# Cross attention on one core: scores issued in 17 visits a group on two sets of three banks, other products cut into 32-column tiles, V in a ring of 18 tiles

## The chip, the cores and the metric

One Trainium2 chip, one NeuronCore. The metric is the device time of one execution in microseconds (us), float32 throughout.

## The reference, cut to what matters

Eight batches; 512 queries, 1593 text keys (padded to 1600) and 8 image tokens; 20 heads of 16 dimensions.

```python
q = split_heads(hidden_states @ w_q)          # (8, 20, 512, 16)
k = split_heads(text @ w_k); v = split_heads(text @ w_v)      # text: (8, 1593, 512)
out_text = softmax(q k^T / sqrt(16)) v
out_ip = softmax(q k_ip^T / sqrt(16) + mask_ip) v_ip          # 8 tokens a batch
out = (out_text + out_ip) @ w_out + b_out + hidden_states
```

## The kernel before, in words

Heads are worked in groups of four (`GH`), five groups a batch, 40 groups in all. K and Q of a group are made in float32, split into a high and a low part by GpSimd, stored to a scratch tensor and loaded again as stacks of 48 rows, two heads on partitions 0 to 47 and two on 64 to 111 (`SIDE`). With these stacks the scores are made twice, with single-pass matmuls (`exact`, float32r).

- **Maxima.** `max_unit` (L540) makes scores with queries on the partitions, one matmul for each side; `take_max` (L851) reduces the pair on VectorE. 32 units of 2 x 400 columns are made for each group, one group ahead. `max_bank` has four banks, so two units are in flight: unit u waits for the reduction of unit u - 2. `negative_parts` (L856) negates the maxima and splits them; `negative_piece` (L494) transposes them on TensorE; `negative_copy` (L728) copies them on ScalarE and issues two DMAs into rows 48 and 49 of `q_stack`, from ScalarE's queue. The next group's exponent scores wait for them (`neg_loaded`, L650).
- **Exponents.** `exp_tile` (L554) makes scores with keys on the partitions, the negated maximum riding along as two more rows, and ScalarE takes the exponent out of PSUM (L741 to L754). 50 tiles a group, two banks. The last two tiles (`k_tail`, L569) use both sides at once.
- **Values.** `pv_tile` (L572) multiplies the four heads' probabilities with `v_ones`, each head in its own 32-column part of the array (17 columns used), 13 key tiles a group. A float32 matmul appears in the trace as two passes, so one `pv_tile` is 8 matmuls.
- **Other products** (`work`, L498) share one bank, `work_bank`: `k_piece` (L440, 64 columns wide, two halves side by side), `q_piece` (L451), `v_piece` (L471, 128 columns wide), `out_piece` (L486), `ip_piece` (L462), the folded image weights (WA, WB) and the transposes TA, TB.

TensorE's order is written by hand. The loop of `body` (L637) goes over 13 key tiles `kt`; each has maximum units, two exponent tiles, maximum units, `pv_tile` of `kt - 1`, two more exponent tiles, maximum units and a share of `work` from `work_plan` (L62). So the array goes from scores to values, back to scores, to other work, and back. All engines run the same plan in order.

- VectorE: reductions, and between them `invert_sums` (L867), which waits for the DMA of the sums, `ip_scale` (L842), `out_add` (L896) and the two halves of the image softmax (L872, L885).
- SyncE's queue, in `body` L397: `normalise` (L353: sums out, reciprocals to scratch, broadcast back), `pack` (L363), and `stack_group` (L342) for the group after next: store K, wait, load K (12 DMAs), store Q, load Q. `normalise` stands ahead of the K loads.
- ScalarE's queue: the four context loads of the next batch (`load_ctx`, L761, 3.3 MB) behind the copy of K piece (4, 1), at visit (2, 3); x after Q piece 4; and the maxima's DMAs at `kt` 12 of each group.
- In the prologue (L602 to L635) K and Q of groups 0 and 1 and the first six V tiles are made, with the 32 maximum units of group 0 beside.

Of the kernel before, what the change touches and what calls it, by code (L numbers as in the profile page):

```python
# [40 lines left out]
QUARTERS = 4  # L41
EXPS = FULL * GH + GH // 2
UNITS = (GH // SIDES) * QT * QUARTERS
BLOCKS = (0, 0, 1)
Q_BLOCKS = (0, 1, 0)
LOADS = SIDES * (2 * len(BLOCKS) + len(Q_BLOCKS))
SCALE = float(DH) ** -0.5
NEG = -10000.0
GRID_W, GRID_H = 32, 16
V_EARLY = 6  # L50


def share(steps, turn):

    n, m = turn
    return range(steps * n // m, steps * (n + 1) // m)


WHOLE = (0, 1)


def work_plan(first, last):  # L62

    turns = {("Q", 2): (0, 0), ("K", 2, 0): (0, 1, 2), ("K", 2, 1): (0, 3, 4), ("IP", 2): (0, 5),
             ("K", 3, 0): (1, 0, 1), ("K", 3, 1): (1, 2, 3), ("Q", 3): (1, 4), ("IP", 3): (1, 5), ("K", 4, 0): (1, 12),
             ("K", 4, 1): (2, 0, 1, 2, 3), ("Q", 4): (2, 4, 5, 6), ("IP", 4): (2, 7), ("WA",): (2, 9), ("WB",): (2, 10, 11),
             ("TA",): (3, 10), ("TB",): (3, 11)}
    turns.update({("V", t): (0, t) for t in range(V_EARLY, KT)})  # L70
    if not first:
        turns.update({("OUT", 0): (1, 6, 7), ("OUT", 1): (1, 8, 9), ("OUT", 2): (1, 10), ("OUT", 3): (1, 11)})
    if not last:
        turns.update({("K", 5, 0): (2, 12), ("K", 5, 1): (3, 0, 1, 2, 3), ("Q", 5): (3, 4), ("IP", 5): (3, 5),
                      ("Q", 6): (3, 6, 7, 8), ("IP", 6): (3, 9), ("K", 6, 0): (3, 12), ("K", 6, 1): (4, 0, 1)})
        turns.update({("V", t): (4, 2 * t + 2, 2 * t + 3) for t in range(V_EARLY - 1)})
        turns["V", V_EARLY - 1] = (4, KT - 1)
    else:

        turns.update({("WB",): (2, 12), ("TA",): (3, 11), ("TB",): (3, 12)})  # L80
    plan = {}
    for piece, (g, *kts) in turns.items():
        for n, kt in enumerate(kts):
            assert (g, kt) not in plan
            plan[g, kt] = (piece, (n, len(kts)))
    return plan
# [6 lines left out]
def ends(turn):  # L93
    return turn is not None and turn[0] == turn[1] - 1

SPLITS = ((("Q", 2), ("K", 2, 0), ("K", 2, 1)), (("K", 3, 0), ("K", 3, 1), ("Q", 3)),
# [6 lines left out]
def work_order(first, last):  # L105

    plan, order = work_plan(first, last), {}
    for g in range(NG):
        for kt in range(KT):
            if kt == NEG_AT and not (last and g == NG - 1):  # L110
                order["NEG", g + 1] = len(order)
# [1000 lines left out]
```

## Time and profile before

| | us |
|---|---|
| runs | 2120.46, 2136.64, 2138.08; median 2136.64 |
| profiled execution, its own time | 2130.14 |
| its span, first to last instruction | 2128.3 |
| mean granted TensorE clock | 0.978 |

The span is what a profile shows; the execution's own time lies 1.8 us above it. In the rows below, PE is TensorE's matmuls and PEld its weight loads, DVE is VectorE, ACT is ScalarE; SPq and ACTq are the instructions that issue DMAs.

### The profile page before, as it was taken

The numbers are of one execution on the slowest core, as the hardware profiler recorded it, in microseconds if no ns is written. First come the engines' busy times: TensorE is split into PE (matmuls) and PEld (weight loads), VectorE is DVE, ScalarE is ACT, GpSimd is POOL, SyncE is SP. The second block draws the span as 40 slices with busy tenths as digits, with TensorE's granted clock in tenths as the row PEclk, the third lists the DMA queues.
The fourth block names the chain that finished last, engine by engine and source line by source line (L and its number), as shares of the span: only waits on it lengthen the run. The fifth ranks groups of instructions, "written<-read, shape, count | busy, mean of one in ns | idle before, by whom it ended". The sixth has DMA issues, their size and how long they took to land.

```text
span 2128.3 us, 31016 instructions
## 1 busy us (share of the span) xinstructions
PE 2011.5 (95%) x12048; PEld 824.6 (39%) x12048; DVE 1341.9 (63%) x1623; ACT 1231.1 (58%) x2364; POOL 275.6 (13%) x314
## 2 busy tenths in 40 slices
PE   4899999997999999999999999999999999999987
PEld 2443334432344333443334433444334443344332
DVE  4757666565665676666755667656766567666660
ACT  0256566555565566555655566655666556665665
POOL 3001111101111011111111111011110111111100
PEclk8999899999999999999999999999999999999999
DMA  7234433353333544435333353333533344443301
GB/s 196 53 53 84 112 67 74 74 117 75 63 76 71 129 81 76 76 66 144 68 70 72 68 141 61 73 61 73 134 66 76 64 119 90 83 77 67 74 21 41
DMA packets 94309, 174.86 MB, mean 82 GB/s; under 512 B 37937, under 2 KB 62386, under 8 KB 90322
## 3 DMA queue, kind: packets, MB, share of 16 engines
q1 hardware_dynamic: 86066, 144.55, 35.1%
q10 hardware_dynamic: 7936, 28.18, 3.9%
q8 instruction: 95, 1.56, 0.3%
q14 instruction: 52, 0.43, 0.1%
q0 software_dynamic: 160, 0.14, 0.1%
HBM read 117.75 MB, written 48.82 MB: 78 GB/s over the span
## 4 chain that ended last, share of the span: by engine, by line
PE 84%; DMA 4%; issue 4%; ACT 4%; DVE 2%; ACTq 1%; SPq 1%; POOL 0%; POOLq 0%
PE pv_bank L580 22%; PE exp_bank L566 19%; PE max_bank L548 14%; PE work_bank L474 10%; PE work_bank L445 10%; PE work_bank L489 3%; PE work_bank L455 3%; DMA q_stack<-neg_rows 3%; ACT probs L754 2%; DVE quarter_max L853 1%; PE work_bank L467 1%; ACT probs_tail L754 1%; ACTq L738 1%; ACTq L763 1%; DMA ctxt<-in_ctx_t 0%
## 5 line engine op out<-in xcount | busy, mean ns | idle before, releaser
L853 DVE TENSOR_REDUCE quarter_max<-max_bank 128x2 f32<-128x800 f32 x1280 | 1232.4, 989 | 692.0 <-PE max_bank L548 687.7
L754 ACT ACTIVATE probs<-exp_bank 128x512 f32<-128x512 f32 x1872 | 1016.2, 595 | 528.3 <-PE exp_bank L566 501.0
L548 PE MATMUL max_bank<-k_stack,q_stack 48*128 48x400 f32 x2560 | 542.7, 384 | 55.9 <-issue 28.2
L566 PE MATMUL exp_bank<-q_stack,k_stack 50*128 50x512 f32 x1872 | 507.3, 469 | 19.9 <-ACT probs L754 19.7
L580 PE MATMUL pv_bank<-probs,v_ones 128*17 128x512 f32 x3840 | 512.5, 606 | 2.0 <-ACT probs L754 2.0
L566 PEld LDWEIGHTS exp_bank<-q_stack,k_stack 50*128 50x128 f32 x1872 | 227.9, 186 | 501.6 <-ACT probs L754 473.5
L548 PEld LDWEIGHTS max_bank<-k_stack,q_stack 48*128 48x128 f32 x2560 | 271.8, 189 | 244.7 <-issue 105.5
L445 PE MATMUL work_bank<-ctxt,wk 128*64 128x400 f32 x1280 | 257.8, 523 | 12.9 <-DMA ctxt<-in_ctx_t 11.1
L474 PE MATMUL work_bank<-wv,ctxt 128*128 128x320 f32 x768 | 246.1, 455 | 0.4 <-ACT neg_rows L698 0.4
L996 POOL TENSOR_TENSOR k_parts<-k_full,zero 128x400 fp32r<-128x400 f32 x80 | 68.2, 852 | 930.4 <-ACT k_full L698 930.4
L474 PEld LDWEIGHTS work_bank<-wv,ctxt 128*128 128x128 f32 x768 | 136.3, 191 | 85.5 <-issue 39.9
L1025 POOL TENSOR_TENSOR o_sum<-o_sum,r_wide 128x512 f32<-128x512 f32 x40 | 51.0, 1276 | 654.0 <-DMA r_wide<-scratch_r 654.0
L698 ACT ACTIVATE v_ones<-work_bank 128x320 f32<-128x320 f32 (+1 forms) x112 | 46.9, 419 | 152.2 <-PE work_bank L474 131.3
L445 PEld LDWEIGHTS work_bank<-ctxt,wk 128*64 128x64 f32 x1280 | 79.2, 139 | 140.4 <-issue 118.0
L580 PEld LDWEIGHTS pv_bank<-probs,v_ones 128*17 128x17 f32 x3840 | 63.8, 95 | 144.8 <-issue 120.7
L698 ACT ACTIVATE k_full<-work_bank 128x400 f32<-128x400 f32 x80 | 40.4, 505 | 135.0 <-PE work_bank L445 135.0
L999 POOL TENSOR_TENSOR k_parts<-k_full,k_parts 128x400 fp32r<-128x400 f32 x80 | 83.1, 1039 | 6.3
L455 PE MATMUL work_bank<-xt,wq 128*64 128x256 f32 (+1 forms) x480 | 72.5, 405 | 0.6 <-ACT k_full L698 0.6
L489 PE MATMUL work_bank<-wout,o_t 128*128 128x320 f32 (+1 forms) x224 | 71.6, 452 | 0.0
L1004 POOL TENSOR_TENSOR q_parts<-q_full,zero 128x256 fp32r<-128x256 f32 x40 | 24.5, 612 | 232.0 <-DMA scratch_q<-q_parts 140.5
L754 ACT ACTIVATE probs_tail<-exp_bank 128x512 f32<-128x512 f32 x78 | 42.3, 596 | 11.5 <-PE exp_bank L569 11.0
L489 PEld LDWEIGHTS work_bank<-wout,o_t 128*128 128x128 f32 (+1 forms) x224 | 39.1, 189 | 24.0 <-issue 12.8
(86 smaller groups left out, 585.4 us busy)
## 6 DMA issues: line engine op xcount, KB each, us to landing
k_stack<-scratch_k SPq DMA_DIRECT2D x240, 200.0 KB, 6.1
scratch_k<-k_parts SPq DMA_DIRECT2D x80, 400.0 KB, 4.7
ctxt<-in_ctx_t ACTq DMA_DIRECT2D x28, 800.0 KB, 9.1
q_stack<-scratch_q SPq DMA_DIRECT2D x240, 64.0 KB, 2.3
scratch_q<-q_parts SPq DMA_DIRECT2D x80, 128.0 KB, 6.7
r_wide<-scratch_r SPq DMA_DIRECT2D x40, 256.0 KB
o_t<-o_sum SPq DMA_DIRECT2D x160, 32.0 KB, 2.0
xres<-in_x SPq DMA_DIRECT2D x8, 640.0 KB, 4.3
```

The costliest lines, as they stand in the source:

```text
L445: last = nc.tensor.matmul(work_bank[half * GR:(half + 1) * GR, 0:CHUNK], wk[:, ct, (g % NG) * GR:(g % NG + 1) * GR], ctxt[:, ct, keys:keys ...
L455: last = nc.tensor.matmul(work_bank[half * GR:(half + 1) * GR, 0:QHALF], wq[0:rows, ct, (g % NG) * GR:(g % NG + 1) * GR], xt[0:rows, ct, h ...
L474: last = nc.tensor.matmul(work_bank[:, 0:D], ctxt[:, ct, t * 128:(t + 1) * 128], wv[:, ct, :], start=(ct == 0), stop=(ct == CT - 1))
L489: last = nc.tensor.matmul(bank, o_t[0:rows, k, t * 128:(t + 1) * 128], wout[0:rows, k, :], start=(k == 0), stop=(k == k_end))
L548: last = nc.tensor.matmul(max_bank[:, (u % 2) * 2 + side, 0:CHUNK], exact(q_stack[stack, slot, c, t * 128:(t + 1) * 128]), exact(k_stack[s ...
L566: nc.tensor.matmul(bank[:, :], exact(k_stack[stack, slot, c, kt * 128:(kt + 1) * 128]), exact(q_stack[stack, slot, c, :]), start=True, sto ...
L580: last = nc.tensor.matmul(pv_bank[h * 32:h * 32 + VW, :], v_ones[:, kt, head * VW:(head + 1) * VW], p, start=(kt == 0), stop=(kt == FULL))
L698: return nc.scalar.activation(dst, src, ACT.Copy)
L754: nc.scalar.activation(dst, exp_place(n, final), ACT.Exp, scale=SCALE).then_inc(probs_ready, 1)
L853: nc.vector.reduce_max(quarter_max[:, :, u // QUARTERS, u % QUARTERS], max_bank[:, (u % 2) * 2:(u % 2) * 2 + 2, 0:CHUNK], AX.X).then_inc(m ...
L996: nc.gpsimd.tensor_tensor(exact(part[:, 0, :]), k_full[:, c, :], zero[:, :].to_broadcast([128, CHUNK]), ALU.add)\
L999: nc.gpsimd.tensor_tensor(exact(part[:, 1, :]), k_full[:, c, :], part[:, 0, :], ALU.subtract).then_inc(k_split, 1)
```

## The change

- The scores of a group go in 17 visits (`VISITS`). A visit makes three exponent tiles on three banks and three maximum tiles of 512 columns on three banks, exponent and maximum by turns on opposite sides. `exp_bank` has three banks, `max_bank` three instead of four, and `begin_round` waits until VectorE has reduced *all* of the round before. A maximum round is one reduction of 3 x 512 (`take_max`); round 0 is `max_rest`, 16 matmuls of 64 columns for the last 64 keys. So 17 rounds a group in place of 32 units.
- Maxima run a group and two rounds ahead (`LEAD`): visit 14 has the last round of the next group, visit 15 the transposition, and visit 15 also round 0 of the group after.
- Behind the scores of a visit come `pv_tile` (in 13 of 17 visits, `PV_AT`) and then the other work, both in 32-column parts of the array: `strips` cuts K, Q, V, OUT, IP, WA, WB, TA, TB to 32 columns, up to four side by side. Transposes become float32 matmuls with the identity; the third step of Q is padded to 128 rows.
- V in a ring of 18 tiles, ten made in the batch before; K made three groups ahead (K 7 in group 4); probabilities in a ring of three.
- SyncE's queue in a group is now: load K of the group after next, `normalise`, `pack`, store and load Q, and last `store_k(group_no + 3)`. K piece (4, 1), and so the context load behind it, ends in visit 14 of group 1. `invert_sums` stands at visit 2 of each group, the softmax halves at (2, 5) and (2, 12).
- The prologue makes K of group 2 and V tiles 0 to 9, with 19 rounds beside.

```diff
+BANKS = 3
+VISITS = FULL * GH // BANKS + 1
+ROUNDS = VISITS
+LEAD = 2
+V_RING = 18
+V_EARLY = 10
+PV_AT = {0: FULL, 2: 0, 3: 1, 4: 2, 6: 3, 7: 4, 8: 5, 10: 6, 11: 7, 12: 8, 14: 9, 15: 10, 16: 11}
+NEG_AT = 15
...
+    put(1, ("K", 4, 0), 4, (11, 2), (12, 2))
+    put(1, ("K", 4, 1), 4, (13, 3), (14, 1))
...
-                    if g or not first:
+                    if group_no + 2 < B * NG:
+                        slot_free(group_no + 2)
+                        load_k(group_no + 2)
+                    if group_no:
                         normalise(group_no - 1)
...
+                    if group_no + 3 < B * NG:
+                        store_k(group_no + 3)
...
+            def strips(rows):
+                return [(at, min(32, rows - at)) for at in range(0, rows, 32)]
...
+                        for at, rows in strips(GR):
+                            dims = (g % NG) * GR + at
+                            last = nc.tensor.matmul(work_bank[half * GR + at:half * GR + at + rows, 0:CHUNK],
+                                                    wk[:, ct, dims:dims + rows], ctxt[:, ct, keys:keys + CHUNK],
+                                                    start=(ct == 0), stop=(ct == CT - 1))
...
+            def begin_round(n, r):
+                if r == 0:
+                    pe.wait_ge(stack_loaded[n % RING], loads_of(n))
+                if n * ROUNDS + r:
+                    pe.wait_ge(max_taken, n * ROUNDS + r)
...
+                    for v in range(VISITS):
+                        n, r = round_at(group_no, v)
+                        if v == 0 or v == VISITS - 1:
+                            if n is not None:
+                                max_round(n, r)
+                            if v == 0:
+                                pe.wait_ge(neg_loaded, (group_no + 1) * 32)
+                            for at in tiles_at(v):
+                                exp_tile(group_no, at)
+                        else:
+                            for k, at in enumerate(tiles_at(v)):
+                                exp_tile(group_no, at)
+                                if n is not None and r:
+                                    if k == 0:
+                                        begin_round(n, r)
+                                    max_tile(n, r, k)
+                            if n is not None and r == 0:
+                                max_round(n, r)
...
+            def take_max(n, r):
+                dve.wait_ge(max_scores, n * EXPS + SIDES + r * BANKS)
...
+                nc.vector.reduce_max(out_at, scores, AX.X).then_inc(max_taken, 1)
```

## Rows read from the trace of the kernel before

**Rows 1.** The page, busy time, share of the span and instructions.

```profile
PE 2011.5 (95%) x12048; PEld 824.6 (39%) x12048; DVE 1341.9 (63%) x1623; ACT 1231.1 (58%) x2364; POOL 275.6 (13%) x314
```

**Rows 2.** Six middle batches (first, last, sum): length, busy times, clock, DMA share, GB/s.

```profile
343.00:610.00 267.00, 250.08 (x1501) 102.31 (x1498) 165.29 (x200) 153.92 (x295) 32.96 (x38) 0.97 0.40 81
...
1626.00:1878.00 252.00, 244.50 (x1492) 100.31 (x1493) 165.25 (x200) 153.20 (x294) 33.08 (x38) 1.00 0.41 85
sum 1535.00, PE 1484.00 PEld 607.58 DVE 991.77 ACT 922.20 POOL 198.22; mean PE 247.33 PEld 101.26 DVE 165.30 ACT 153.70 POOL 33.04
```

**Rows 3.** Groups of instructions: busy us, mean ns of one, idle before.

```profile
L853 DVE TENSOR_REDUCE quarter_max<-max_bank 128x2 f32<-128x800 f32 x1280 | 1232.4, 989 | 692.0 <-PE max_bank L548 687.7
L754 ACT ACTIVATE probs<-exp_bank 128x512 f32<-128x512 f32 x1872 | 1016.2, 595 | 528.3 <-PE exp_bank L566 501.0
...
L880 DVE TENSOR_REDUCE ip_max<-s_ip 128x80 f32<-128x640 f32 x8 | 6.6, 820 | 0.3
```

**Rows 4.** TensorE's waits: us in total, times, longest.

```profile
PE max_bank L548 <- DVE quarter_max L853: 12.4, 15, 1.2
```

**Rows 5.** Timeline, one key tile with a K piece: start us, us, what.

```profile
885.34 1.56 PE L445 MATMUL work_bank<-ctxt,wk 128*64 128x400 f32 x8
...
886.83 0.46 PE L548 MATMUL max_bank<-k_stack,q_stack 48*128 48x400 f32 x2
...
887.12 0.40 PE L566 MATMUL exp_bank<-q_stack,k_stack 50*128 50x512 f32 x2
...
887.36 0.35 PE L548 MATMUL max_bank<-k_stack,q_stack 48*128 48x400 f32 x2
...
887.64 1.05 PE L580 MATMUL pv_bank<-probs,v_ones 128*17 128x512 f32 x8
...
888.63 0.57 PE L566 MATMUL exp_bank<-q_stack,k_stack 50*128 50x512 f32 x2
```

**Rows 6.** Timeline, a V tile and the matmul behind it.

```profile
892.50 2.42 PE L474 MATMUL work_bank<-wv,ctxt 128*128 128x320 f32 x8
...
894.86 0.46 PE L548 MATMUL max_bank<-k_stack,q_stack 48*128 48x400 f32 x2
```

**Rows 7.** Timeline, scores to reduction (two places), and reduction to scores.

```profile
1005.53 0.34 PE L548 MATMUL max_bank<-k_stack,q_stack 48*128 48x400 f32 x2
...
1005.92 0.99 DVE L853 TENSOR_REDUCE quarter_max<-max_bank 128x2 f32<-128x800 f32 x1 [0.60 <-PE max_bank L548]
...
64.76 2.79 DVE L853 TENSOR_REDUCE quarter_max<-max_bank 128x2 f32<-128x800 f32 x3 [0.50 <-PE max_bank L548]
65.81 0.19 PEld L548 LDWEIGHTS max_bank<-k_stack,q_stack 48*128 48x128 f32 x2 [1.24 <-DVE quarter_max L853]
```

**Rows 8.** Timeline, SyncE's queue, last K loads and behind them; then a sums DMA alone.

```profile
901.68 1.35 SPq L329 DMA_DIRECT2D k_tail<-scratch_k  x3
903.08 1.23 SPq L310 DMA_DIRECT2D scratch_q<-q_parts  x2
910.20 1.95 SPq L339 DMA_DIRECT2D q_stack<-scratch_q  x2
...
2080.18 1.93 DMA sums<-o_sum
```

**Rows 9.** Context loads: from issue to landing.

```profile
DMA to landing us min/median/max: 4.9/8.5/14.2
```

**Rows 10.** Timeline, one group whose stack came late, with the idle time before.

```profile
508.65 0.70 PE L548 MATMUL max_bank<-k_stack,q_stack 48*128 48x400 f32 x2 [9.76 <-issue]
```

**Rows 11.** Timeline, where the parts of the kernel begin: V, exponents, the end.

```profile
59.20 2.50 PE L474 MATMUL work_bank<-wv,ctxt 128*128 128x320 f32 x4
...
91.85 0.39 PE L566 MATMUL exp_bank<-q_stack,k_stack 50*128 50x512 f32 x2
...
2107.70 0.59 SPq L356 DMA_DIRECT2D sums<-o_sum  x1
```

**Rows 12.** Timeline, 80 short matmuls in a row.

```profile
22.91 3.24 PE L589 MATMUL work_bank<-probs 128*64 128x64 f32 x80 [0.87 <-DMA probs<-in_w_v_ip]
```

More of the change, by code:

```diff
@@ L108, in work_order @@
     for g in range(NG):
-        for kt in range(KT):
-            if kt == NEG_AT and not (last and g == NG - 1):
+        for v in range(VISITS):
+            if v == NEG_AT and not (last and g == NG - 1):
                 order["NEG", g + 1] = len(order)
-            piece, turn = plan.get((g, kt), (None, None))
+            piece, turn = plan.get((g, v), (None, None))
             if begins(turn):
@@ L532, in work @@
                     for t in range(QT):
-                        last_mm = nc.tensor.transpose(work_bank[:, t * 128:(t + 1) * 128], p_ip[:, t, 0:128], ident_f[:, :])
+                        for at, rows in strips(128):
+                            last_mm = nc.tensor.matmul(work_bank[at:at + rows, t * 128:(t + 1) * 128],
+                                                       p_ip[:, t, at:at + rows], ident_f[:, :], start=True, stop=True)
                     last_mm.then_inc(work_full, 1)
@@ new lines, in max_tile @@
+            def max_tile(n, r, k):
+                i, slot = (r - 1) * BANKS + k, n % RING
+                side, at, chunk = i % SIDES, i // (SIDES * CHUNKS), i // SIDES % CHUNKS
+                c, t = at // QT, at % QT
+                stack = slice(side * SIDE, side * SIDE + STACK)
+                nc.tensor.matmul(max_bank[:, k, :], exact(q_stack[stack, slot, c, t * 128:(t + 1) * 128]),
+                                 exact(k_stack[stack, slot, c, chunk * WIDE:(chunk + 1) * WIDE]),
+                                 start=True, stop=True).then_inc(max_scores, 1)
@@ new lines, in max_rest @@
+            def max_rest(n):
+                slot = n % RING
+                for at in range(PAIRS):
+                    c, t = at // QT, at % QT
+                    for side in range(SIDES):
+                        stack = slice(side * SIDE, side * SIDE + STACK)
+                        mm = nc.tensor.matmul(max_bank[:, side, at * TAIL:(at + 1) * TAIL],
+                                              exact(q_stack[stack, slot, c, t * 128:(t + 1) * 128]),
+                                              exact(k_stack[stack, slot, c, CHUNKS * WIDE:KEYS]), start=True, stop=True)
+                        if at == PAIRS - 1:
+                            mm.then_inc(max_scores, 1)
@@ L600, in ip_values @@
                 last.then_inc(work_full, 1)
-            units = iter(range(UNITS))
+            rounds = iter(range(ROUNDS + LEAD))
             pe.wait_ge(wk_loaded, 16)
@@ L945, in _ @@
             dve.wait_ge(mask_step, step + 3)
-            units = iter(range(UNITS))
+            rounds = iter(range(ROUNDS + LEAD))
             for piece, turn, beside in PRO_PLAN:
@@ L984, in _ @@
             for t in range(QT):
[L985 removed]
+                out_add(B, t, end + t, out_place(t))
         @block.gpsimd
@@ L1043, in _ @@
                 split_q(g, PRO_ORDER["Q", g])
+            for c in range(2):
+                split_k(2, c, PRO_ORDER["K", 2, c])
             def body(b, first, last):
```

483 lines of the change are left out of this document (243 added, 240 removed).

## Prediction

> **What bounds the kernel now.** I read the page's busy times first: TensorE 95%, VectorE 63%, ScalarE 58% [rows 1]. Then the same by batches: in the middle six TensorE is busy 247 of 256 us. An undisturbed one is 252 us long; the first of the six is 267 us, some 10 of them lost at one late stack [rows 2, 10]. TensorE's waits say the same from the other side: it waited for VectorE's reductions 12.4 us in all [rows 4]. So TensorE's order of work is the kernel, and every idle stretch that the change opens in it is paid in full.
>
> The timeline shows what TensorE's time is made of [rows 5]. Scores: a first pair of 400 columns starts at 886.83, a pair of 512 at 887.12, the next at 887.36, the values at 887.64. A pair of 512 columns therefore takes 0.24 us from start to start; the first one after a change of form 0.10 more (its weights are not loaded ahead), and on leaving 0.10 more (the array empties). The values: 887.64 to 888.63, 0.99 us, of which two passes of 512 columns stream 0.43 us each and about 0.13 is again entering and leaving. K: 0.33 us a pass (1.49 us for four passes and the switch). V: 2.36 us for 8 passes, 0.27 each and 0.2 at the ends [rows 6]. Each key tile pays four such switches, some 0.2 us each.
>
> **What the change takes from TensorE.** The streamed columns stay the same: four 32-column tiles side by side move at the rate of the values' four. Per middle batch of 85 visits I get:
> - scores: a visit has three pairs of 512 columns, 0.33 + 0.24 + 0.33 = 0.90 us. Visit 15 has the rest round, eight pairs of 64 columns limited by their 128-column weights at 0.11 each, 1.6 us; visit 16 the tails, 1.3 us. 15 x 0.90 + 2.9 = 16.4 a group, 82 us;
> - values 65 x 0.85 = 55.5;
> - K 40 steps x 0.67 = 26.7, V 52 x 0.53 = 27.7, output 16 x 0.53 = 8.5, Q 15 x 0.43 = 6.4, the small ones 7;
> - entering and leaving the 32-column form once a visit, 85 x 0.13 = 11.
>
> Sum 225 us against 252: 11% less. What it could cost more: four times as many instructions. 80 matmuls with their loads ran at 0.04 us each [rows 12]; a K step is 8 in 0.67 us, a V step 8 in 0.53, so their issue is covered; only TA, TB and IP may be issue bound (under 1 us a batch either way).
>
> The Trainium skill (TensorEngine Tiling (Array Packing), Key Properties) says that changing the tiling mode drains the array; the 0.10 us on leaving the scores [rows 5] agrees.
>
> **The wait that is added.** Before, a unit waited for the reduction two units back. Now `begin_round` waits for the reduction of the round just before: all three banks are filled, reduced, and only then filled again. The cycle, from rows: after VectorE's end TensorE's next load starts 0.06 us later (65.75 to 65.81, [rows 7]); weights and two further matmuls of the same side until the third maximum starts, 0.11 + 2 x 0.23 = 0.57; from a matmul's start to VectorE's, 0.39 at 400 columns (1005.53 to 1005.92, [rows 7]), 0.43 at 512; the reduction: 800 elements take 0.989 us [rows 3], 0.83 of it at 0.96 elements per ns and 0.16 fixed, so 1536 take 1.76. Sum 2.8 us. Bounds on the reduction: 1.60 without its fixed part, 1.90 in proportion to the 800.
>
> Visits last 225 / 85 = 2.64 us on average, but unevenly: a visit with only values or only two small steps has 1.9 to 2.5 us of work, one with four steps 3.2 or more, visits 15 and 16 3 to 4. In-order issue means that nothing is caught up: whatever is behind the first maximum (the values and the work of that visit) waits too. Walking the 85 visits with this recurrence gives idle time of 5.8, 3.6, 6.7, 4.6 and 4.2 us in the five groups (the 6.7 has 1.8 at (2, 7), where the softmax, three operations of 0.82 us [rows 3], holds back a reduction). 225 + 25 = 250 us: nearly all of the gain is gone.
>
> The Trainium skill (Perfetto Trace Analysis, Optimizing Scalar/DVE Operations) speaks against this edit: where VectorE isn't saturated but causes bubbles on other engines, instructions should be broken up; here they are merged. VectorE at 63% [rows 1] is such a case, and by this rule too TensorE gets bubbles.
>
> **Two transfers behind others in a queue.** (a) SyncE now issues the 12 K loads ahead of the sums. Twelve issues take 5.4 us (1.35 for three, [rows 8]); a store issued behind them let its waiter go at 910.20, 7.1 us after its issue at 903.08, while a sums DMA alone takes 1.9 [rows 8]. VectorE waits for the sums at visit 2, 8.4 us into the group, and behind it stands the reduction that the maxima of visit 4 need. K loads can begin once the group before has made its last scores, 2 us before the group, where K was stored early (groups 3, 4, 0): sums there at 9 to 10 us, 0.7 us lost each. After group 0 K is stored late (piece (3, 1) ends at visit 14): 2.9 us lost in group 1. Bounds a group: 0 if the sums overtake, 5 if they take the full 7 us.
> (b) The context load now is issued at the end of visit 14 of group 1, and the next thing on ScalarE's queue is the DMA of the maxima of group 2, in visit 15. The last of four context loads lands up to 14.2 us after its issue [rows 9]. If a queue serves in order, the maxima land 15 to 16 us after visit 14; TensorE wants them 6 us after it (visits 15, 16 and three maxima). 9 to 10 us idle in seven batches; bounds 1 (no order: ScalarE is still 2 us late by issuing the four) and 12. I take 9.7: the least and the largest landing of the four loads, 4.9 and 14.2 us [rows 9], look like a queue, and a late stack can cost as much, 9.76 us [rows 10]. In the batch with that stop the granted clock was 0.97, in the undisturbed one 1.00 [rows 2]: 3% of a batch is 7 us, the nearest row for a stop of this length; I take 3 us a batch, since the low clock partly falls on idle time.
>
> The Trainium skill (DMA: Bandwidth & Descriptors, Two DMAs through the same engine are not ordered) says that within a queue of one DMA engine descriptors start in order; no row here shows a small DMA behind the context load.
>
> **The sum.** A middle batch: 250 + 2 (groups 3, 4, 0) + 2.9 + 9.7 + 3 + 1.5 of other waits = 269 us. Prologue: values of V start near 58 as now [rows 11]; 17 rounds of 2.8 us, then the negated maxima and two more visits, 58 + 47 + 8 = 113 us until the first exponent, against 92. Last batch: 49, 49, 50, 45 and a last group bound by ScalarE, 50 x 0.595 [rows 3] = 30, with 10 of late sums and 3 of the rest: 237. The end is as before, 21 us from the sums [rows 11] and 2 ahead of them. 113 + 7 x 269 + 237 + 23 = **2256 us**, against the profiled 2130, which lies 0.3% under the median of the runs.
>
> **Rivals.**
> - *No queue effect* (sums and maxima overtake the loads): batches of 254, 113 + 7 x 254 + 228 + 23 = 2142. For it: the 16 DMA engines are only 41% busy [rows 2]. Against: the 7.1 us behind the K loads. Chance 0.14.
> - *TensorE stays the bound*, the other side: the three reductions hide under values and work. It decides at a loop of 2.64 us, 0.16 less than I add up, or if exponent tiles absorb the wait; with 225 + 6 a batch: 105 + 7 x 231 + 215 + 23 = 1960. For it: VectorE's total falls, 17 reductions of 1.7 against 32 of 1. Against: the loop leaves at most 1.9 us of each 2.8 to VectorE, and light visits can't borrow. Chance 0.16.
> - *The tiles don't do what they say*: 32-column pieces of K, V and output run two abreast, not four. That doubles 63 us a batch: 8 x 63 on top of the forecast, above 2700. The values' eight matmuls in 0.99 us speak against it. Chance 0.03.
> - *More of (a) and (b)*: 12 us in (b) and 5 in each group for (a), 20 us more a batch: 2400. Chance 0.07.
>
> The forecast itself, 2190 to 2340, has 0.60; without half of (a) and (b) it is the lower end, with three fifths of the last rival's 20 us the upper. A difference of 1% is about what a measurement of this kernel can tell from none. Slower by over 1%: 0.60 + 0.03 + 0.07 and a small part of the first rival, 0.73; within: 0.10; faster 0.17. The range: 2085 to 2380, which takes in the first rival and most of the last, and leaves out the second and third, 0.19.
>
> **What would show it.** TensorE's waits: maxima for VectorE's reduction some 150 to 200 us in all, in most visits 0.2 to 0.9 us each; visits in the timeline never under 2.8 us; segments of V in 2.14 us without ends; reductions of 1.75 us. Once a batch, at the start of group 2, a stop of near 10 us for the maxima's DMA, and at visits 2 to 4 of group 1 VectorE idle for the sums. Wrong would be: TensorE busy over 95% again, no stop at group 2, a visit of 2.4 us.

## Result: 2330 us, 9.3% slower, and the profile after

The changed kernel takes 2329.9 us (median of 4 runs, 2328.3 to 2335.3) against 2135.7 (2120.5 to 2138.1) in the same comparison: ratio 1.093, 95% interval 1.088 to 1.098. The forecast was 2256 in a range of 2085 to 2380, so 5.6% slower where it is 9.3%. The profiled execution spans 2326.9 us. Here and below a time is the median of the fast runs; the one slow run (2620.2 us, of the last experiment) is left out. The page of the profiled execution, against [rows 1], first busy times, then the granted clock in 40 slices:

```profile
PE 2082.4 (89%) x17944; PEld 829.8 (36%) x17944; DVE 1294.7 (56%) x1025; ACT 1223.8 (53%) x2364; POOL 281.0 (12%) x314
...
PEclk9998999999999899998999899998999989999777
```

TensorE fell from 95% to 89% of a longer span. Its busy time rose by 71 us although the streamed columns are the same. Part of the stream ran at the lower clock: the mean granted clock of the run is 0.938, against 0.978 before. VectorE and ScalarE lost share too, so every engine now waits.

The middle batches, from first exponent to first exponent (the first of six, and the sum of the six; columns as in [rows 2]):

```profile
380.65:659.53 278.88, 254.40 (x2233) 102.05 (x2231) 158.90 (x125) 152.65 (x296) 33.77 (x38) 0.95 0.37 77
...
sum 1664.24, PE 1519.50 PEld 610.59 DVE 953.39 ACT 916.82 POOL 202.64; mean PE 253.25 PEld 101.76 DVE 158.90 ACT 152.80 POOL 33.77
```

A batch takes 277.4 us (1664.24 / 6) where an undisturbed one took 252 [rows 2], and the forecast had 269. TensorE is busy 253.3 of it and idle 24.1; the granted clock of the six lies between 0.95 and 0.97.

TensorE's waits, the place of [rows 4], and VectorE's for the sums:

```profile
PEld max_bank L596 <- DVE tile_max L918: 207.1, 272, 5.5
DVE recips L935 <- DMA sums<-o_sum: 171.8, 39, 35.4
PE max_bank L596 <- DVE tile_max L918: 110.0, 175, 5.2
PE exp_bank L632 <- DMA q_stack<-neg_rows: 50.2, 9, 7.6
```

The first and third row are one wait, seen by the weight load and by the matmul: where [rows 4] had 12.4 us for TensorE, there are 110. The stops for the sums, below, are in these 110 too, since what TensorE then waits for is a reduction. The other two are the two transfers of the forecast.

Now the timeline of a group 1, visits 2 to 4. The single wait a round, as it repeats:

```profile
716.00 0.56 PE L596 MATMUL max_bank<-k_stack,q_stack 48*128 48x512 f32 x2
...
717.01 1.76 DVE L918 TENSOR_REDUCE tile_max<-max_bank 128x3 f32<-128x1536 f32 x1 [0.54 <-PE max_bank L596]
...
718.82 0.19 PEld L596 LDWEIGHTS max_bank<-k_stack,q_stack 48*128 48x128 f32 x2 [0.22 <-DVE tile_max L918]
718.82 0.51 PE L596 MATMUL max_bank<-k_stack,q_stack 48*128 48x512 f32 x2
```

From 716.00 to 718.82 is the loop: 2.82 us with a reduction of 1.76 in it, as added up. In the last two rows the weight load waited 0.22 us, while the matmul shows no idle time: a part of this wait is hidden in TensorE's busy time. And the stop for the sums behind it:

```profile
718.56 0.60 SPq L381 DMA_DIRECT2D sums<-o_sum  x1
...
724.18 0.25 DVE L935 RECIPROCAL recips<-sums 128x16 f32<-128x16 f32 x1 [5.41 <-DMA sums<-o_sum]
724.35 1.70 DVE L918 TENSOR_REDUCE tile_max<-max_bank 128x3 f32<-128x1536 f32 x1
...
726.10 0.80 PE L596 MATMUL max_bank<-k_stack,q_stack 48*128 48x512 f32 x2 [4.37 <-DVE tile_max L918]
```

VectorE stands 5.41 us at the reciprocal with a reduction of maxima ready behind it, and TensorE stands 4.37 at the maxima that need that reduction. The stretches before and after it (length, busy times, granted clock):

```profile
711.00:721.30 10.30, 10.30 (x97) 4.12 (x93) 5.76 (x4) 7.25 (x15) 0.00 (x0) 1.00 0.90 123
726.10:729.50 3.40, 3.40 (x17) 1.31 (x21) 1.72 (x1) 1.08 (x2) 0.00 (x0) 0.50 0.27 93
729.50:733.00 3.50, 3.50 (x30) 1.25 (x26) 0.68 (x3) 0.65 (x2) 1.27 (x1) 0.64 0.09 32
```

Ahead of the stop the clock is granted in full (2.4 GHz), behind it half (1.2 GHz) for 3.4 us and partly for 3.5 more. Over those 6.9 us this costs 3.4 x 0.50 + 3.5 x 0.36 = 3.0 us of TensorE's work. By this estimate a stop of 4.4 us costs over 7.

Last, the start of group 2:

```profile
764.19 1.24 SPq L336 DMA_DIRECT2D scratch_k<-k_parts  x2
...
765.58 1.30 ACTq L800 DMA_DIRECT2D q_stack<-neg_rows  x2
...
774.58 1.22 PE L632 MATMUL exp_bank<-q_stack,k_stack 50*128 50x512 f32 x3 [6.88 <-DMA q_stack<-neg_rows]
774.66 1.23 SPq L358 DMA_DIRECT2D k_stack<-scratch_k  x3
...
780.12 0.59 SPq L381 DMA_DIRECT2D sums<-o_sum  x1
```

The maxima let TensorE go 9.0 us after their issue. The K store, issued in the same two microseconds on the other queue, lets the K loads go 10.5 us after its own.

### The profile page after: what moved, and what is told of

The parts are those of the page before. It is cut to its first block, busy times and chain, and to the rows that moved or that the text cites. A ratio compares the mean times of both kernels' runs of the same rounds, so it can differ in the third digit from the quotient of the medians.

```text
span 2326.9 us, 42217 instructions
## 1 busy us (share of the span) xinstructions
PE 2082.4 (89%) x17944; PEld 829.8 (36%) x17944; DVE 1294.7 (56%) x1025; ACT 1223.8 (53%) x2364; POOL 281.0 (12%) x314
## 4 chain that ended last, share of the span: by engine, by line
PE 55%; DMA 17%; DVE 13%; SPq 9%; issue 3%; POOL 1%; ACT 1%; POOLq 0%; ACTq 0%
PE pv_bank L648 13%; DMA sums<-o_sum 11%; DVE tile_max L918 11%; PE exp_bank L632 11%; PE max_bank L596 11%; PE work_bank L475 9%; PE work_bank L508 6%; DMA scratch_k<-k_parts 5%; SPq L361 4%; SPq L358 4%; PE work_bank L524 2%; PE max_bank L607 1%; POOL k_parts L1066 1%; POOL k_parts L1063 1%; PE exp_bank L636 1%
## 5 line engine op out<-in xcount | busy, mean ns | idle before, releaser
L918 DVE TENSOR_REDUCE tile_max<-max_bank 128x3 f32<-128x1536 f32 (+1 forms) x680 | 1173.0, 1725 | 801.0 <-PE max_bank L596 769.5
L596 PE MATMUL max_bank<-k_stack,q_stack 48*128 48x512 f32 x1920 | 596.2, 464 | 110.6 <-DVE tile_max L918 110.0
L632 PE MATMUL exp_bank<-q_stack,k_stack 50*128 50x512 f32 x1920 | 600.3, 451 | 52.3 <-DMA q_stack<-neg_rows 50.2
L632 PEld LDWEIGHTS exp_bank<-q_stack,k_stack 50*128 50x128 f32 x1920 | 273.7, 196 | 420.1 <-ACT probs L817 208.2
L475 PE MATMUL work_bank<-ctxt,wk 128*32 128x400 f32 x2560 | 257.7, 507 | 21.1 <-DMA ctxt<-in_ctx_t 11.0
L508 PE MATMUL work_bank<-wv,ctxt 128*32 128x320 f32 x3072 | 254.6, 445 | 15.3 <-DVE s_ip L904 14.2
L508 PEld LDWEIGHTS work_bank<-wv,ctxt 128*32 128x32 f32 x3072 | 97.1, 112 | 175.8 <-issue 73.6
L475 PEld LDWEIGHTS work_bank<-ctxt,wk 128*32 128x32 f32 x2560 | 77.7, 111 | 186.2 <-issue 162.0
L1071 POOL TENSOR_TENSOR q_parts<-q_full,zero 128x256 fp32r<-128x256 f32 x40 | 24.5, 611 | 664.3 <-ACT q_full L757 661.0
L817 ACT ACTIVATE probs_tail<-exp_bank 128x512 f32<-128x512 f32 x80 | 43.4, 595 | 94.5 <-PE exp_bank L636 85.8
L524 PE MATMUL work_bank<-wout,o_t 128*32 128x320 f32 (+1 forms) x928 | 80.3, 467 | 0.0
L486 PE MATMUL work_bank<-xt,wq 128*32 128x256 f32 x960 | 71.0, 401 | 1.2 <-ACT k_full L757 1.2
```

Source lines behind the costliest of these rows:

```text
L475: last = nc.tensor.matmul(work_bank[half * GR + at:half * GR + at + rows, 0:CHUNK], wk[:, ct, dims:dims + rows], ctxt[:, ct, keys:keys + C ...
L508: last = nc.tensor.matmul(work_bank[at:at + rows, 0:D], ctxt[:, ct, key:key + rows], wv[:, ct, :], start=(ct == 0), stop=(ct == CT - 1))
L524: last = nc.tensor.matmul(bank[at:at + rows, :], o_t[0:deep, k, t * 128 + at:t * 128 + at + rows], wout[0:deep, k, :], start=(k == 0), sto ...
L596: nc.tensor.matmul(max_bank[:, k, :], exact(q_stack[stack, slot, c, t * 128:(t + 1) * 128]), exact(k_stack[stack, slot, c, chunk * WIDE:(c ...
L632: nc.tensor.matmul(bank[:, :], exact(k_stack[stack, slot, c, kt * 128:(kt + 1) * 128]), exact(q_stack[stack, slot, c, :]), start=True, sto ...
L817: nc.scalar.activation(dst, exp_bank[:, at % BANKS, :], ACT.Exp, scale=SCALE).then_inc(probs_ready, 1)
```

## Experiments

"A batch" below is the mean of the six middle ones in the run's profile. The changed kernel: first exponent at 102.1, a batch 277.4, last batch 257.5. The kernel before, run beside each set of experiments, had medians of 2133 to 2140 us; between experiments of different sets a difference under 10 us shows nothing by itself.

**The sums ahead of the K loads.**

```diff
-                    if group_no + 2 < B * NG:
-                        slot_free(group_no + 2)
-                        load_k(group_no + 2)
                     if group_no:
                         normalise(group_no - 1)
+                    if group_no + 2 < B * NG:
+                        slot_free(group_no + 2)
+                        load_k(group_no + 2)
```

> The sums' DMA is issued ahead of the 12 K loads again, as before the change; nothing else differs from the changed kernel. If the late sums (landing 7 us after issue behind the loads) hold VectorE and through it TensorE, they now land about 1.9 us after issue, the visits 3 and 4 of each group fall to the loop's 2.8 to 3.1 us, and 1.6 us in each of groups 3, 4 and 0, 6.7 in group 1 and 4 in group 2 go: 15 us a batch, 2210 us in all. Rival A: it is the loop alone that holds those visits, then less than 15 us go. Rival B: the K loads, now issued behind the sums' whole round trip, come too late for the next group's maxima, then the time rises above 2330.

Measured 2183.4 us (2179.1 to 2186.0), 1.019 of the kernel before (1.017 to 1.022); a batch 259.4. The gain, 147 us, is more than the 120 expected, 18.0 us a batch and not 15; the clock of the whole run rose from 0.938 to 0.963. In the six middle batches together:

```profile
sum 1556.47, PE 1475.68 PEld 605.27 DVE 953.60 ACT 916.67 POOL 202.51; mean PE 245.95 PEld 100.88 DVE 158.93 ACT 152.78 POOL 33.75
```

TensorE is busy 246.0 us a batch and not 253.3, and idle 13.5 and not 24.1, at a granted clock of 0.98. So of the 18.0 us some 10.7 were idle time, and 7.3 the same work at the lower clock. In a group 1 the reciprocal now starts with no idle time before it, right behind a reduction:

```profile
676.42 1.76 DVE L918 TENSOR_REDUCE tile_max<-max_bank 128x3 f32<-128x1536 f32 x1 [0.55 <-PE max_bank L596]
678.10 0.24 DVE L935 RECIPROCAL recips<-sums 128x16 f32<-128x16 f32 x1
```

Rival A falls, as more than 15 us a batch went. Rival B falls as well: the K loads behind the sums are in time.

**The sums as late, but VectorE at them later.** `INVERT_AT = 2` becomes `INVERT_AT = 6`, all else as in the changed kernel.

> The changed kernel, queue orders as it has them, but VectorE inverts the sums at visit 6 of a group, not at visit 2: the sums stay as late as they are, only VectorE's reductions no longer stand behind the wait. If the price of the late sums is VectorE's wait and nothing else, the time is that of the run with the sums issued first, 2183, or up to 20 us over it; the DMA of the sums still lands some 7 us after its issue. Rival: the late sums cost by what follows them (scaling, packing, the next store and load of Q), or the K loads ahead are what cost; then it stays near 2330.

Measured 2182.0 us (2181.6 to 2191.2), a batch 259.4: the same as with the sums first. As ratios to the kernel before the two are 1.025 (1.022 to 1.028) and 1.019, so they agree to 0.6%. In a group 1 the sums' DMA is issued as late as ever, and nothing waits:

```profile
679.72 0.60 SPq L381 DMA_DIRECT2D sums<-o_sum  x1
...
691.29 0.24 DVE L935 RECIPROCAL recips<-sums 128x16 f32<-128x16 f32 x1
```

So the price of the late sums is VectorE's wait with the reductions queued behind it, and within 0.6% nothing after it. Two unlike edits, one on SyncE's queue and one number in VectorE's order, give the same 147 us.

**The context load behind the maxima's DMA.**

```diff
                         if v == NEG_AT and group_no + 1 < B * NG:
                             negative_copy(...)
+                            if g == 1 and not last:
+                                load_ctx(b + 1)
...
                             k_copy(b * NG + piece[1], piece[2], number)
-                            if piece == ("K", 4, 1) and not last:
-                                load_ctx(b + 1)
```

> The context load is issued one visit later, behind the DMA of the maxima of group 2 on ScalarE's queue; nothing else differs from the changed kernel. If the context load is what makes the maxima late, they land in 2.6 us as in the other groups, the stop at the start of group 2 goes (7 us with the late last visit of group 1, in seven batches, and up to 3 us of clock): 2260 to 2280 us. Rival: the maxima are late because all 16 DMA engines are full with K loads and stores, whichever queue they are on; then their landing stays near 9 us and the time within 10 us of 2330.

Measured 2357.3 us (2349.8 to 2364.9), 1.101 of before (1.098 to 1.104, the changed kernel 1.093): 27 us slower than the changed kernel, a batch 281.7, neither what the theory nor what its rival said. The stop at the start of group 2 did shrink, the last visit of group 1 from 9.5 to 5.5 us. But visit 3 of group 2 now took 13 to 15 us:

```profile
1064.31 0.62 SPq L381 DMA_DIRECT2D sums<-o_sum  x1
1077.63 0.25 DVE L935 RECIPROCAL recips<-sums 128x16 f32<-128x16 f32 x1 [10.92 <-DMA sums<-o_sum]
```

The context load and the 12 K loads are now under way together, and the sums behind the K loads land 13.3 us after their issue. The stop moved from one small transfer to the other.

**Both orders undone.** The two diffs above together.

> Both queue orders undone. If the two costs are separate, their gains add: about 2150 us, and what is left against the kernel before (2136) is the loop of one wait per round and the longer prologue. Rival: the two stops cover each other or something else becomes late behind them, then it stays over 2200.

Measured 2156.1 us (2153.1 to 2162.9), 1.008 of before (1.005 to 1.010), as expected; a batch 254.8. With the sums out of reach, moving the context load gives 27 us, as many as it cost without. The two gains are not separate: that of the second edit changes its sign with the first.

This order has a smaller stop of its own, which is not for a transfer:

```profile
710.02 4.40 ACTq L826 DMA_DIRECT2D ctxt<-in_ctx_t  x4
...
715.27 1.19 PE L632 MATMUL exp_bank<-q_stack,k_stack 50*128 50x512 f32 x3 [2.83 <-ACT probs_tail L817]
```

ScalarE spends 4.40 us on issuing the four context loads, and the last exponents of group 1 stand behind it. TensorE waits 2.83 us for them at the start of group 2, in each of seven batches.

**The maxima by another queue.** On top of the sums' order, the DMA of the maxima is issued by SyncE (ScalarE only copies them out of PSUM), the context load staying at visit 14; first behind the store of K:

```diff
                         store_k(group_no + 3)
+                    if group_no + 1 < B * NG:
+                        sp.wait_ge(work_empty, number(("NEG", g + 1)) + 1)
+                        for side in range(SIDES):
+                            ...
+                            sp.dma_start(q_stack[...], neg_rows[...]).then_inc(neg_loaded, 16)
```

> As the run with the sums issued ahead of the K loads (2183), the context load at its place at visit 14, but the DMA of the maxima goes by SyncE's queue, behind the store of K, and not by ScalarE's behind the context load. If what makes the maxima late in group 2 is that they stand behind the context load in one queue, they land in 3 to 5 us, the last visit of group 1 falls from 9.5 to 5 or 6 us and the time to about 2156 us, as with the context load issued behind them. Rival: the 16 DMA engines are full with the context load whichever queue it came by; then the maxima land near 9 us still, and the time stays near 2183.

Measured 2193.1 us (2188.8 to 2194.9), a batch 260.4: no gain. The maxima land as late as on ScalarE's queue, 8.9 us from issue to matmul. But the store of K stood ahead of them, so that the place in a queue was not excluded. The second time the same lines stand ahead of the store:

> As the run with the maxima's DMA on SyncE's queue (2193), but issued ahead of the store of K, so that nothing large stands ahead of it in its own queue; the context load is issued 4 us earlier by ScalarE's queue. If the place in a queue decides, the maxima of group 2 now land in 3 to 4 us, the last visit of group 1 takes 5 to 6 us and the time is about 2156 to 2165 us. If the 16 DMA engines are simply full with the context load, they land 7 to 9 us after issue, that visit stays over 9 us and the time stays at 2185 to 2200 us.

Measured 2171.4 us (2166.3 to 2174.4), between the two, 12 us less than with ScalarE's queue (2183.4). As ratios, 1.017 (1.011 to 1.022) and 1.019 (1.017 to 1.022), the two can't be told apart; but a batch is 257.4 and not 259.4. Both runs in the timeline, first behind the store, then ahead of it:

```profile
718.07 1.24 SPq L336 DMA_DIRECT2D scratch_k<-k_parts  x2
719.36 1.43 SPq L456 DMA_DIRECT2D q_stack<-neg_rows  x2
...
728.28 1.22 PE L639 MATMUL exp_bank<-q_stack,k_stack 50*128 50x512 f32 x3 [6.70 <-DMA q_stack<-neg_rows]
```

```profile
716.67 1.45 SPq L454 DMA_DIRECT2D q_stack<-neg_rows  x2
718.16 1.29 SPq L336 DMA_DIRECT2D scratch_k<-k_parts  x2
...
724.08 1.22 PE L639 MATMUL exp_bank<-q_stack,k_stack 50*128 50x512 f32 x3 [5.31 <-DMA q_stack<-neg_rows]
```

With nothing large ahead in its own queue the small DMA still needs 7.4 us from issue to matmul. The last visit of group 1 takes 9.5 us behind the context load, 7.9 ahead of the K store, 5.5 with the context load behind. The place in the queue is worth the first 1.6 us. The other 2.4 aren't all the transfer's: with the context load ahead, ScalarE copies the maxima 1.9 us after the last matmul of their transposition has started, held up by issuing the loads (2.1 to 2.2 us); with the load behind it is 0.3 us. By an estimate from these, 1.6 us of the 5.31 that TensorE waits above are the late copy, and 3.7 the landing, though nothing large stood ahead in the queue. Nor is 5.5 a visit without a stop, since the 2.83 us for ScalarE are in it. By the Trainium skill (DMA: Bandwidth & Descriptors, Issuing engines are not separate DMA queues) transfers from any issuing engine run on the same 16 DMA engines and interleave; the slow landing on a queue of its own agrees.

**One reduction a bank.** Queue orders as in the changed kernel.

```diff
                 stack = slice(side * SIDE, side * SIDE + STACK)
+                pe.wait_ge(max_taken, n * TAKES + (1 if r == 1 else 1 + (r - 2) * BANKS + k + 1))
                 nc.tensor.matmul(max_bank[:, k, :], ...
...
-                nc.vector.reduce_max(out_at, scores, AX.X).then_inc(max_taken, 1)
+                    for k in range(BANKS):
+                        at = i % (SIDES * CHUNKS) + k
+                        dve.wait_ge(max_scores, n * EXPS + SIDES + i + k + 1)
+                        nc.vector.reduce_max(flat[:, at:at + 1], max_bank[:, k, :], AX.X).then_inc(max_taken, 1)
```

> Each round's reduction is cut into three of 512 elements, one a bank, and TensorE waits for a bank's own reduction only; queue orders as in the changed kernel. If the single wait a round (the loop of 2.8 us) holds light visits, visits with 2 us of work now take 2.2 us, and 20 us a batch go: about 2180 us, although VectorE has 34 instructions more a group and about 0.3 us more work a visit (3 x 0.69 = 2.08 against 1.73). Rival A: VectorE's instructions are the limit, then nothing goes or the time rises. Rival B: the late sums and maxima take over what the loop leaves (they stand on the same path); then only half goes, 2250 us.

Measured 2190.3 us (2187.1 to 2193.7), 1.023 of before: 140 us less, where 150 were expected. That the total fits is partly luck: a batch takes 264.9 us, 12.5 less and not 20. The first exponent at 94.5 (7.6 earlier) and the last batch of 225.4 (32 shorter) make up for it. In the middle batches the stops for the sums take up part of the gain, as rival B had it: visit 3 of the groups 0 and 2 to 4 takes 5.2 to 6.9 us (medians), where it took 4.2 to 4.8.

**All three together.**

> Both queue orders undone and each round's reduction cut into three, one a bank. If the late sums and maxima and the one wait a round are together all that stands between the changed kernel and its TensorE work (225 us a batch worked out), a middle batch now takes 230 to 237 us, the first exponent comes at 94.5 as with the cut reductions alone, and the whole takes 1965 to 2000 us, well under the kernel before. Rival: TensorE's work, with four times as many instructions in 32-column pieces, is itself some 240 to 250 us a batch, then 2050 to 2110.

Measured 1945.7 us (1938.2 to 1947.4), ratio to the kernel before 0.914, 95% interval 0.911 to 0.917. It beats both kernels. First exponent at 93.1, a batch 231.9, last batch 207.7. Its page, a middle batch, the group of reductions and the wait that is left:

```profile
PE 1880.2 (97%) x17944; PEld 762.1 (39%) x17944; DVE 1365.4 (70%) x2305; ACT 1195.5 (61%) x2364; POOL 281.9 (14%) x314
```

```profile
1480.89:1712.81 231.92, 228.76 (x2233) 92.99 (x2231) 167.76 (x285) 149.19 (x296) 33.94 (x38) 0.99 0.47 93
```

```profile
L598 PE MATMUL max_bank<-k_stack,q_stack 48*128 48x512 f32 x1920 | 621.8, 442 | 5.0 <-DVE tile_max L921 3.2
```

TensorE waits 3.2 us for reductions in the whole kernel, though VectorE does three instructions where it did one, and 71 us more in all. TensorE is the bound again, at 97%. The run to compare with is the one with both orders undone, whose wait and middle batches are:

```profile
PE max_bank L596 <- DVE tile_max L918: 66.4, 145, 2.7
```

```profile
sum 1528.80, PE 1473.82 PEld 604.52 DVE 953.65 ACT 916.31 POOL 202.55; mean PE 245.64 PEld 100.75 DVE 158.94 ACT 152.72 POOL 33.76
```

A batch falls from 254.8 to 231.9, by 22.9 us, at the same granted clock of 0.99. Only 6.0 of them were shown as idle time (9.2 and 3.1 a batch); 16.9 stood in TensorE's busy time, 245.6 and 228.8. The same visit in both, exponent and maximum, first with one wait a round, then with one a bank:

```profile
878.69 0.50 PE L632 MATMUL exp_bank<-q_stack,k_stack 50*128 50x512 f32 x1
879.09 0.50 PE L596 MATMUL max_bank<-k_stack,q_stack 48*128 48x512 f32 x2
```

```profile
793.64 0.50 PE L634 MATMUL exp_bank<-q_stack,k_stack 50*128 50x512 f32 x1
793.64 0.73 PE L598 MATMUL max_bank<-k_stack,q_stack 48*128 48x512 f32 x2
```

The maximum starts 0.40 us behind the exponent in one and with it in the other, and neither shows idle time. The list of waits understates a short wait that recurs.

What the prediction draws from the Trainium skill (Perfetto Trace Analysis, Optimizing Scalar/DVE Operations), that an unsaturated engine which causes bubbles elsewhere should have its instructions broken up, is what these rows show.

**What the 32-column pieces are worth.** In that fastest version `strips` returns `[(0, rows)]`.

> As the run before it in this list, with K, Q, V, output and the small products undivided again (one matmul of 64 or 128 columns of weights where there were two or four of 32). If the 32-column pieces save only switches of the array's form (0.13 to 0.2 us in each of some 78 visits a batch that have other work), this costs 10 to 16 us a batch: 80 to 130 us over that run. Rival A: the pieces save nothing, the same within 10 us. Rival B: the pieces cost (their issue is not covered), then this one is faster.

Measured 2037.2 us (2030.1 to 2044.5): 91 us more, a batch 243.8 and not 231.9, so 11.9 us for 85 visits. It is still 96 us under the kernel before (2133.2): of the 187 us that the fastest version gains, the pieces give about a half, and the visits and the prologue the rest. The same visit in both, values, a K step and the next scores; with the pieces, then without:

```profile
748.92 1.05 PE L650 MATMUL pv_bank<-probs,v_ones 128*17 128x512 f32 x8
749.79 0.85 PE L476 MATMUL work_bank<-ctxt,wk 128*32 128x400 f32 x8
750.58 0.50 PE L634 MATMUL exp_bank<-q_stack,k_stack 50*128 50x512 f32 x1
```

```profile
783.35 1.05 PE L650 MATMUL pv_bank<-probs,v_ones 128*17 128x512 f32 x8
784.33 0.89 PE L476 MATMUL work_bank<-ctxt,wk 128*64 128x400 f32 x4
785.15 0.49 PE L634 MATMUL exp_bank<-q_stack,k_stack 50*128 50x512 f32 x1
```

Values to K takes 0.87 us within one form of the array and 0.98 across two; the K step itself 0.79 against 0.82. That is 0.14 us in this visit; in each of 85 it would be the 11.9.

**The pieces alone, in the kernel before.** `k_piece`, `v_piece` (but for the tail) and `out_piece` divided as in the change.

> The kernel before, with only K, V and output divided into 32-column pieces. TensorE is the bound there, and the values and the other work of a key tile follow each other, so one switch of form of 0.1 to 0.2 us goes in some 55 key tiles a batch: 2140 - 8 x (6 to 11) = 2050 to 2090 us. Rival: no effect (within 10 us), or slower by the issue of four times as many instructions.

Measured 2126.9 us (2114.2 to 2142.6), ratio 0.998 (0.995 to 1.001): no effect. The timeline says why: in the kernel before, the other work follows exponent and maximum scores, not the values. It is entered and left across a change of form either way, and 0.07 us is all that a V step of 2.36 [rows 6] gains:

```profile
880.91 0.40 PE L556 MATMUL max_bank<-k_stack,q_stack 48*128 48x400 f32 x2
881.24 2.36 PE L481 MATMUL work_bank<-wv,ctxt 128*32 128x320 f32 x32
883.53 0.50 PE L574 MATMUL exp_bank<-q_stack,k_stack 50*128 50x512 f32 x2
```

**The values moved next to the work, in the kernel before**, behind the key tile's last two exponent tiles, with the pieces and without (the diff shows the order that results):

```diff
-                        if kt:
-                            pv_tile(group_no, g, kt - 1)
-                        ...
                         if kt < FULL:
                             exp_tile(group_no, kt, 2)
                             exp_tile(group_no, kt, 3)
                         next_units(places[2])
+                        if kt:
+                            pv_tile(group_no, g, kt - 1)
+                        ...
                         if (g, kt) in plan:
```

> The kernel before with 32-column pieces for K, V and output (alone they changed nothing, 0.998), and with the values of a key tile moved behind its last two exponent tiles, so that the other work follows them at once. If a 32-column piece saves a switch only where it follows the values, this takes two boundaries of 0.10 to 0.19 us out of some 60 key tiles a batch: 8 x 60 x 0.2 to 0.3 = 100 to 140 us less than before, 1995 to 2040 us, if no new wait eats it. Rival: the pieces do nothing in this kernel whatever the order, because it is not TensorE's time that they save; then it equals the run with the move alone.

> The kernel before with that move alone, work undivided. One boundary fewer (scores, values, work, scores in place of scores, values, scores, work, scores): 8 x 60 x 0.10 to 0.15 = 50 to 70 us less than before, 2070 to 2090 us. Rival: the values later in the tile hold back ScalarE's next exponents, which wait for the buffer that the values free, then no gain or slower. Against the run with the pieces, the difference is the price of the switch between 32-column and wide work, 0.15 to 0.19 us in each of 50 to 60 key tiles a batch, 60 to 90 us.

Measured 2524.9 us (2503.1 to 2533.9) with the pieces and 2572.9 (2552.6 to 2583.6) without, 18% and 21% slower than before. Both expectations of a gain were wrong. The rival of the second has the outcome right and not the wait: it is TensorE that waits for ScalarE's exponents, once in most key tiles, 240 us in all, where it was 20. The likely reason, not tried apart, is that the values had given ScalarE the time for the exponents that free the two exponent banks. From the run with the pieces:

```profile
1006.46 0.98 PE L574 MATMUL exp_bank<-q_stack,k_stack 50*128 50x512 f32 x2 [0.50 <-ACT probs L762]
...
1007.56 1.05 PE L588 MATMUL pv_bank<-probs,v_ones 128*17 128x512 f32 x8
1008.43 0.85 PE L450 MATMUL work_bank<-ctxt,wk 128*32 128x400 f32 x8
```

Values to K is 0.87 us here too, the price within one form. Between the two runs the pieces are worth 48 us, where next to the scores they were worth nothing measurable. Because of the new wait this pair is weak evidence by itself; the switch is priced by the pair before.

## Why the prediction was right in direction and short in size

The span is 70.9 us above the forecast of 2256. By parts: first exponent at 102.1 and not 113, -11; seven batches in 1942.8 us (102.1 to 2044.9) and not 7 x 269 = 1883, +60; last batch 257.5 and not 237, +20.5; end 24.5 and not 23, +1.5.

The runs cut a batch of 277.4 us into 231.9 that stay when everything else is undone, 22.9 for the single wait a round (254.8 - 231.9), 4.6 for the context load's place (259.4 - 254.8) and 18.0 for the sums (277.4 - 259.4). This holds in that order of undoing alone: one reduction a bank gives 12.5 us with both orders as in the change, and moving the context load alone costs 4.3.

Against the forecast's terms that is +3.3 us for the work and its loop (254.8 for 251.5), +13.1 for the sums (18.0 for 4.9) and -8.1 for the context load and its clock (4.6 for 12.7): 8.4 in all. That the forecast came as close as it did is in part luck, since the two transfers were missed in opposite directions.

- **TensorE's work, 225 us a batch: right.** The version without the waits takes 231.9, of which 228.8 busy, 3% more than added up. That is the rival "TensorE stays the bound" with its 225 + 6 and 1960 us, which was right about the work and wrong about the wait.
- **The added wait, 2.8 us a round and 25 a batch: right.** The loop measured 2.82, the cost 22.9. The waits for reductions, 150 to 200 us in the forecast, are listed as 110 with the stops for the sums and as 66.4 without both stops, because most of the wait is counted as busy time. "Visits never under 2.8 us" was wrong as it was put. From a round's first maximum to the next one's, the middle of the kernel shows none under 2.57 us and half within 2.78 to 2.86; the 2.58 at visit 0 is the same loop with its three maxima together and no exponents between them. From first exponent to first exponent visits 0 and 1 take 1.98 and 2.15. The 250 us worked out and the 254 of the rival without queue effects stand against 254.8 with both orders undone.
- **Term (a), the sums behind the K loads, 0.7 us in groups 3, 4, 0 and 2.9 in group 1: the step that failed.** With the sums first the groups 0 to 4 of a batch, from first exponent to first exponent, shrink by 2.4, 7.0, 4.6, 2.0 and 2.0 us (means of six), 18.0 a batch where I had 4.9. In groups 3, 4 and 0 I had the sums there 9 to 10 us into the group; VectorE took them at 10.2 to 10.6, 7.0 to 7.4 after their issue behind the K loads, and each stop cost 2.0 to 2.4 us and not 0.7. In group 1 I had the K loads' late start, but not what it does to TensorE: the stop of 4.4 us and the clock behind it. In group 2 I had put nothing and given no reason for it. It cost 4.6 us: the stop of (b) delays the K store and loads too, so that the sums come late once more (issued at 780.12, 5.5 us into the group). The upper bound of 5 us a group doesn't hold in group 1 (7.0); summed, 25 a batch, it does.
- **Term (b), 9.7 us at group 2 and 3 of clock: oversized, and its mechanism mostly wrong.** The stop is there (6.9 to 7.6 us), but undoing it gives 4.6 us a batch, because behind the maxima the issuing of the context load brings the stop of 2.83 us for ScalarE's exponents. And the place in ScalarE's queue decides only 1.6 us. Another 1.6 are ScalarE's late copy, which I had in the lower bound only (2 us late by issuing the four). The rest is slow landing on whatever queue. I had argued from landings of 4.9 to 14.2 us, which queueing and sharing both explain.
- **Clock.** I charged 3 us a batch to the stop at group 2 alone. The stops for the sums had the larger surcharge: without them TensorE is busy 7.3 us a batch less for the same columns, at a granted clock of 0.98 and not 0.95 to 0.97. With the context load moved as well the clock is 0.99, but the busy time falls by only 0.3 more.
- **Prologue, 113 us: 11 too much.** The first V piece started at 43.7 us, not at 58 as before the change, since no rounds stand among the pieces ahead of it. From there to the negated maxima at 91.8 were 48 us for the 47 worked out, which fits by chance: the rounds took 2.58 us each (reductions at 56.12, 58.70, 61.28 and on), since no exponents stand between their maxima, and the first reduction began only at 48.1. To the first exponent it was 10 more for the 8.
- **Last batch, 237 us (its terms add up to 236): 20 short.** Groups 1 and 2 took 58.0 and 61.4 and not 49 and 50, 20 us over where I had set aside 10 for late sums. Group 3 took 51.8 and not 45: with little other work its visits fall to the loop, which I had not walked through there; with one reduction a bank, queue orders unchanged, it took 35.6. The last group took 35.2 and not 30, at a granted clock of 0.77.

The first rival (sums and maxima overtake the loads, 2142) is what the run with both orders undone made of it by other means, 2156. That the pieces run two abreast is excluded: a K step of 8 matmuls of 32 columns takes 0.79 us, where the 4 wide ones of the same work take 0.82.

What stays open: why a queue of its own buys a small DMA no more than 1.6 us, and why the clock that moving the context load gives back (0.98 to 0.99) hardly shows in TensorE's busy time.

## What to carry to other kernels

Where an engine waits for one of its small inputs in program order, ask what is queued behind that wait and move the consumer or the transfer: here a single number in VectorE's order was worth 147 us, as much as the order of SyncE's queue. A merged reduction over all the banks that its producer needs next is a loop without overlap; one reduction a bank cost 71 us more of VectorE's time and, once the two stops were gone, took 23 us a batch out of TensorE's. Three quarters of these had been counted as TensorE's busy time, so a short list of waits doesn't clear such a loop. And a good edit can measure as nothing or as a loss while another stop takes up its gain, so test suspects in pairs as well as alone: the context load's move cost 27 us alone and gained 27 beside the other.

## What the runs showed of the hardware that was not expected

- A DMA of 8 KB, issued 2.6 us behind the last of four loads (3.3 MB together) by the other engine's queue, with nothing large ahead of it in its own, released TensorE 7.4 us after issue; behind a store on its own queue 8.9, behind the loads themselves 9.0. A queue of its own bought 1.6 us.
- Issuing DMAs takes the engine's own time: four context loads took ScalarE 2.1 to 2.2 us with the loads ahead of the maxima and 4.4 with them behind, and its copies and exponents stood behind them.
- With one wait a round, 16.9 of the 22.9 us a batch that the wait cost were shown as busy time of TensorE.
- A stop of 4.4 us in TensorE was followed by 3.4 us at half the clock and 3.5 at 0.64, some 3 us of work.
- The 32-column form is worth 0.11 us where it follows 32-column work: 91 us in one order of the work. Where the work stood between wide scores it was worth 6 us, within the measurement's noise (0.998 of before, 0.995 to 1.001).
